# One VectorE instruction in place of two per expert tile: gate times up on GpSimd from a ScalarE copy, tanh written into the bank

## What is computed

```python
g = einsum('btd,edf->ebtf', x, gate_w)      # F = 192
u = einsum('btd,edf->ebtf', x, up_w)
h = silu(g) * u
expert_out = einsum('ebtf,efd->ebtd', h, down_w)
out = einsum('ebtd,bte->btd', expert_out, combine)
```

```python
state = state * exp(dt * A) + (dt * u) * B
y = einsum('bdn,bn->bd', state, C)
```

## Time and profile before

| | |
|---|---|
| median of 3 runs | 1610.0 us (1607.82 to 1610.88) |
| profiled execution, its own time | 1611.76 us |
| its span | 1610.0 us |
| mean granted TensorE clock | 0.925 of full speed |
| busy in the span | TensorE 87%, VectorE 59%, ScalarE 43%, GpSimd 47% |

### The profile page before, as it was taken

How to read it: one execution, slowest core, us unless ns; L and a number is a source line. 1 busy time by engine, 2 the same in 40 slices (tenths; PEclk the granted TensorE clock), 3 DMA queues, 4 the chain that set the end, 5 groups by cost and what they waited for, 6 DMA issues and landing times.

```text
span 1610.0 us, 18778 instructions
## 1 busy us (share of the span) xinstructions
PE 1396.8 (87%) x6080; PEld 1030.1 (64%) x6080; DVE 949.6 (59%) x1234; ACT 689.8 (43%) x1255; POOL 754.2 (47%) x559
## 2 busy tenths in 40 slices
PE   6988982599889889888175999999999999999998
PEld 3535531566556556555165787878788787878786
DVE  2767767999999999999584224241423224241413
ACT  4445433356666665665143333333333333333332
POOL 0000000877778778783631444444544445444542
PEclk9898895699999999999555999999999999999999
DMA  3202215477977887862664910020000100010000
GB/s 104 107 31 75 106 54 194 152 251 236 300 269 253 284 272 229 290 198 80 215 216 169 376 56 0 0 66 1 13 0 0 65 13 0 0 52 0 0 0 26
DMA packets 78200, 191.28 MB, mean 119 GB/s; under 512 B 10856, under 2 KB 15752, under 8 KB 77120
## 3 DMA queue, kind: packets, MB, share of 16 engines
q1 hardware_dynamic: 64832, 157.03, 28.5%
q0 software_dynamic: 6400, 20.98, 4.7%
q10 hardware_dynamic: 6912, 12.59, 2.1%
HBM read 152.55 MB, written 38.01 MB: 118 GB/s over the span
## 4 chain that ended last, share of the span: by engine, by line
PE 57%; DVE 25%; issue 9%; ACT 3%; DMA 3%; POOL 2%; ACTq 0%; SPq 0%; DVEq 0%; POOLq 0%
PE decay L1668 22%; PE bank L1657 21%; DVE decay L1235 14%; PE decay L1423 2%; PE bank L1467 2%; DVE XH L1102 2%; PE bank L1527 1%; PE bank L1487 1%; PE bank L1554 1%; PE bank L1430 1%; PE decay L1477 1%; DVE S L1244 1%; PE decay L1473 1%; PE bank L1437 1%; DVE HH L1255 1%
## 5 line engine op out<-in xcount | busy, mean ns | idle before, releaser
L723 POOL TENSOR_TENSOR S<-DTU,Bb 128x1024 f32<-128x1024 f32 x128 | 303.2, 2387 | 105.0 <-PE bank L1527 69.9
L1380 DVE CAST HFH<-HF 128x512 fp32r<-128x512 f32 x128 | 58.9, 460 | 497.2 <-ACT HF L1033 497.2
L805 POOL TENSOR_TENSOR W2L<-W2R,W2H 128x512 fp32r<-128x512 f32 x128 | 172.5, 1347 | 348.1 <-ACT W2H L1028 348.1
L1235 DVE TENSOR_TENSOR_SCAN decay<-decay,S 128x1024 f32<-128x1024 f32 x128 | 292.9, 2288 | 1.7 <-ACT decay L882 1.6
L1657 PE MATMUL bank<-XSH,W1H 128*128 128x512 f32 x512 | 203.4, 397 | 4.2 <-POOL W1L L801 4.2
L1668 PE MATMUL decay<-W2H,HFH 128*128 128x512 f32 x512 | 200.4, 391 | 5.0 <-DVE HFL L1382 5.0
L1657 PE MATMUL bank<-XSH,W1L 128*128 128x512 f32 x512 | 203.2, 397 | 0.0
L1657 PE MATMUL bank<-XSL,W1H 128*128 128x512 f32 x512 | 202.6, 396 | 0.0
L1668 PE MATMUL decay<-W2L,HFH 128*128 128x512 f32 x512 | 199.9, 390 | 0.0
L1668 PE MATMUL decay<-W2H,HFL 128*128 128x512 f32 x512 | 199.6, 390 | 0.0
L801 POOL TENSOR_TENSOR W1L<-W1R,W1H 128x512 fp32r<-128x512 f32 x128 | 171.0, 1336 | 47.7 <-ACT W1H L1019 47.7
(11 more groups left out here) (211 smaller groups left out, 2071.0 us busy)
## 6 DMA issues: line engine op xcount, KB each, us to landing
WGU<-in_L_ffn_gate_w SPq DMA_DIRECT2D x48, 384.0 KB
WGU<-in_L_ffn_up_w SPq DMA_DIRECT2D x48, 384.0 KB
WD<-in_L_ffn_down_w SPq DMA_DIRECT2D x48, 384.0 KB
Bb<-bc_rows SPq DMA_DIRECT2D x32, 512.0 KB, 6.5
Cb<-bc_rows SPq DMA_DIRECT2D x32, 512.0 KB, 8.6
expert_rows<-YT ACTq DMA_DIRECT2D x48, 256.0 KB
W1R<-in_L_ffn_w SPq DMA_DIRECT2D x6, 1024.0 KB, 13.7
W2R<-in_L_ffn_w SPq DMA_DIRECT2D x6, 1024.0 KB, 14.2
```

Of the source, the lines that this page charges most:

```text
L723: pool.tensor_tensor(S[u % NP][:], DTU[:, ds(b, 1), c, :].to_broadcast([P, PAIR, L]), Bb[j][:], ALU.mult).then_inc(dbu_ready, 1)
L805: pool.tensor_tensor(W2L[f % 2][:], W2R[:, ds(e, 1), f, :].rearrange("p e d -> p (e d)"), W2H[f % 2][:].bitcast(F32), ALU.subtract).then_i ...
L1235: dve.tensor_tensor_scan(flat, flat, S[u % NP][:].rearrange("p i l -> p (i l)"), 0.0, ALU.mult, ALU.add).then_inc(scan_done, 1)
```

## The change

- Buffers TG and HH (128x192 each, two of each) go; GU (128 x 2 x 192, two of it) comes: half 0 for the gate, half 1 for the up part.
- ScalarE, in `tanh_g`: it copies all 384 columns of UP to GU, waits for its own copy, and then writes tanh(g/2) over the gate columns of UP itself instead of into TG.
- GpSimd, new `gate_by_up(j)` behind the `dbu` of `units(j)` and ahead of the gather of tile j+2: it waits for that copy and multiplies g by u in GU (128x192, in place).
- VectorE: `gate_h` goes. `finish_h` waits for the tanh and for GpSimd's product, computes (UP + 1) * GU into GU, and stands between the scan and the read-out of the second unit, where `gate_h` stood; nothing of the experts stands behind that read-out.
- The factor 0.5 moves to the copy of DOWN into YT, which becomes an activation with scale 0.5.
- `turn_h` reads GU's half 0.

```diff
+            def gate_by_up(j):
+
+                pool.wait_ge(gu_copied, j + 1)
+                pool.tensor_tensor(GU[j % 2][:, 0], GU[j % 2][:, 0], GU[j % 2][:, 1], ALU.mult).then_inc(gg_ready, 1)
...
             for j in range(SLOT_TILES):
                 for u in units(j):
                     dbu(*bu(u))
+                gate_by_up(j)
                 if j + 2 < SLOT_TILES:
                     gather(0, j + 2)
...
             def tanh_g(j0, n):
                 act.wait_ge(up_ready, j0 + (n + 3))
-                act.activation(TG[n % 2][:], UP[:, 0:F], ACT.Tanh, scale=0.5).then_inc(tg_ready, 1)
+                act.copy(GU[n % 2][:].rearrange("p g f -> p (g f)"), UP[:, 0:2 * F]).then_inc(gu_copied, 1)
+                act.wait_ge(gu_copied, j0 + (n + 1))
+                act.activation(UP[:, 0:F], UP[:, 0:F], ACT.Tanh, scale=0.5).then_inc(tg_ready, 1)
...
-                act.copy(YT[:], DOWN[:]).then_inc(yt_ready, 1)
+                act.activation(YT[:], DOWN[:], ACT.Copy, scale=0.5).then_inc(yt_ready, 1)
...
-            def gate_h(j0, n):
+            def finish_h(j0, n):
 
                 dve.wait_ge(tg_ready, j0 + (n + 1))
-                dve.scalar_tensor_tensor(TG[n % 2][:], TG[n % 2][:], 1.0, UP[:, 0:F], ALU.add,
-                                         ALU.mult).then_inc(gg_ready, 1)
-
-            def finish_h(j0, n):
-
                 dve.wait_ge(gg_ready, j0 + (n + 1))
-                dve.scalar_tensor_tensor(HH[n % 2][:], TG[n % 2][:], 0.5, UP[:, F:2 * F], ALU.mult,
+                dve.scalar_tensor_tensor(GU[n % 2][:, 0], UP[:, 0:F], 1.0, GU[n % 2][:, 0], ALU.add,
                                          ALU.mult).then_inc(hh_ready, 1)
...
-            gate_h(0, 0)
             finish_h(0, 0)
             for j in range(SLOT_TILES):
                 for i, u in enumerate(units(j)):
                     scan(*bu(u))
                     if i == 1 and j + 1 < SLOT_TILES:
-                        gate_h(0, j + 1)
+                        finish_h(0, j + 1)
                     read_out(*bu(u))
-                    if i == 1 and j + 1 < SLOT_TILES:
-                        finish_h(0, j + 1)
```

More of the change, by code:

```diff
@@ L227, in build_program @@
         gcol = [sb(f, f"gcol{i}", [P, 1], I32) for i in range(2)]
-        TG = [sb(f, f"TG{i}", [P, F]) for i in range(2)]
-        HH = [sb(f, f"HH{i}", [P, F]) for i in range(2)]
+        GU = [sb(f, f"GU{i}", [P, 2, F]) for i in range(2)]
         HT = [sb(f, f"HT{i}", [FH, 2, P]) for i in range(2)]
@@ L375, in build_program @@
         gated = sem("gated")
+        gu_copied = sem("gu_copied")
         gt_ready = sem("gt_ready")
@@ L1558, in turn_h @@
             def turn_h(j0, n, last):
-                hh = HH[n % 2][:].rearrange("p (q k) -> p k q", k=2)
+                hh = GU[n % 2][:, 0].rearrange("p (q k) -> p k q", k=2)
                 pe.wait_ge(hh_ready, j0 + (n + 1))
```

## The result

The kernel with the change took **1597.2 us** (median of 6 runs, 1592.28 to 1601.36) against 1610.1 for the kernel before on the same chip (6 runs, 1607.82 to 1611.81). The ratio is 0.9922, 95% interval 0.9902 to 0.9942. The forecast was 1601.6, range 1596 to 1611. A second set of runs gave 0.9932 (0.9911 to 0.9952). A ratio here is not the quotient of the two medians: in the second set the medians, 1600.4 and 1609.1, differ by 8.7 us, which is 0.5%. So the kernel is faster by 0.5 to 0.8%, some 9 to 13 us where 8.4 were forecast.

A forecast was written before the change was run, and what follows sets the result against it. The prediction took VectorE, in the stage with scan and experts, to set the pace. Its terms, 12.0 - 2.3 - 1.35 = 8.35 us, took the median from 1610.0 to 1601.6 us, range 1596 to 1611.

The forecast's parts named there:

- The gain per tile: VectorE, units with a tile: freeing the place behind the read-out saves 0.25 us for each of 48 tiles, 12.0 us.
- the rival by busy time: VectorE: the instruction taken out brings its whole 0.34 us, 16.3 us before losses, giving 1597.3 us; chance 0.12.
- The prices of the new work: ScalarE's copy 0.47 us, GpSimd's product 0.68 (bounds 0.25 and 1.34), copy to finish 1.21 with handovers.
- Tile 1: Stage start: VectorE's finish stands 3.1 us for GpSimd's product, late behind a dbu; net loss 2.3 us.
- Tile 24: A store holds ScalarE, leaving 0.36 us between tanh and gate against 1.21 needed; 0.85 us lost.
- The few other tiles: Tiles with less than the usual 2.44 to 2.97 us of room before VectorE's finish; 0.5 us allowed together.
- The gather at nothing: GpSimd's gather, issued later behind the product, is late in the slowest cases only, by about 1 us; costed at nothing.
- ScalarE's copy at nothing: ScalarE gets some 24 us more work, covered by its 110.8 us of waiting for VectorE; otherwise a decay comes 0.5 later.
- Sum: Whole kernel: 12.0 gained, less 2.3 at the start and 1.35 at other tiles, gives 8.35 us.

The follow-up runs named there:

- experiments with more products: Changed kernel with one or two more 128x192 products per tile on GpSimd, results unused: 1598.3 us with one, 1614.8 us with two.
- The second copy: Changed kernel with ScalarE's copy of 384 columns from UP to GU made twice per tile: 1607.9 us, ratio 0.9988 to the kernel before.
- finish behind: Changed kernel with finish_h moved behind the read-out instead of between scan and read-out: 1604.2 us, ratio 0.9964 to the kernel before.
- early product: Changed kernel with GpSimd's product of tile 1 alone made ahead of that tile's last dbu: 1599.6 us, ratio 0.9933; repeated, 1597.2 us, 0.9927.
- gathers ahead: Changed kernel with the gather of tile j+2 ahead of the product of tile j in GpSimd's queue: 1603.4 us, ratio 0.9963.
- both moves: Changed kernel with tile 1's product ahead of that tile's last dbu and every gather ahead of the product on GpSimd: 1601.9 us, ratio 0.9950.

## Why the prediction was right, and where its steps missed

**The gain per tile: right.** 0.25 was forecast from start-to-start times, 0.26 came (3.84 to 3.58), and the rival by busy time, 0.34 and 16.3 us, is out: an instruction behind the read-out costs 0.27, one between scan and read-out 0.12, one in each 0.39. The prediction set against this the rule of the Trainium skill, "VectorE: DVE Perf Modes", section "The DRAIN you can't avoid", that the next instruction does not start until the pipe is empty, by which each instruction would be worth its whole duration. It left out that the same paragraph goes on: a next one that is not held starts earlier. The trace agrees with that second sentence: the finish, which has no wait for the scan, starts 2.19 us after a scan of 2.29.

**The prices of the new work: right.** Copy 0.48 (0.47 forecast), product 0.59 (0.68), from copy to finish at the five tiles where VectorE waited or nearly did 1.25 (1.21). GpSimd's round is 15.9 us and VectorE's 17.5, and the experiments with more products put the edge between a round of 17.2, which cost nothing in the median, and one of 18.4.

**Tile 1: right in place, the size set by the clock.** 3.1 us were forecast and 4.16 came. TensorE's up products took 5.31 us there against 4.44 in the profile that the forecast was read from, and the sums for which the last `dbu` waits come behind them. In the profiles with the product behind the tile's units and the finish in the gap the unit lost 1.5 to 4.7 us, 1.5 where the clock stayed up. The net loss at the start was forecast at 2.3; VectorE reaches unit 12 46.7 us after its first scan, before the change 44.6, so 2.1 late, and 2.6 with the half microsecond that two tiles should have brought. That this is near the forecast is luck in part, for the two profiles had different clocks there.

**Tile 24: right in place, and its size goes with the store.** A store held ScalarE ahead of this tile's copy in both profiles of the changed kernel, for 1.72 and 2.86 us, where it was 3.76 before:

```profile
528.32 0.60 ACT L912 ACTIVATE YT<-bank 128x512 f32<-128x512 f32 x1 [1.72 <-DMA expert_rows<-YT]
```

```profile
532.66 0.60 ACT L912 ACTIVATE YT<-bank 128x512 f32<-128x512 f32 x1 [2.86 <-DMA expert_rows<-YT]
```

The first used up all slack: the product ended 0.1 us ahead of the finish, and the unit took 3.65, so it lost 0.07. In the second profile the unit took 4.79 and lost 1.20, where it lost 1.06 in the kernel before. Twelve of the thirteen profiles with the change or a variant of it have a wait for the store there, of 0.2 to 2.9 us. It is a property of the kernel, and its length one of the run.

**The few other tiles: named too small.** 0.5 us were allowed. In the first profile tiles 6, 14, 22 and 38 lost 2.8 together, in the second tiles 6, 14, 18, 32 and 40 lost 5.1. The kernel before lost 2.8 at tiles 2, 8 and 32.

**The gather at nothing: right for the time, wrong for the wait.** It was late 15 times, not in the slowest cases only. Taking that away brought nothing.

**ScalarE's copy at nothing: the step that was least sound.** I named as cover the 110.8 us that ScalarE waits for VectorE, and as the one price a decay 0.5 later. The second copy shows another way: the take-out of the sums comes later, TensorE waits, and its next h and up come late. A second 0.5 us a tile costs 7 to 10.5 us of stage without any decay being late. The changed kernel's own wait at tile 22 (0.79) stands at the end of the same way; how much of its 7 and 11 us of waits in all (4 before) the first copy has by it was not separated.

**Sum.** In the stage 8.35 us were forecast, and 9.6 and 6.2 came in two profiles. The gain in the places was 47 x 0.26 = 12.2, where 12.0 were forecast, and the waits took back 7.3 - 3.9 = 3.4 and 10.6 - 3.9 = 6.7, where 3.65 were. That the 3.4 is so near is luck in part, since it came at other tiles than those that were priced. Another 0.7 came in both profiles at the units without a tile. The medians moved by 12.9 and 8.7. Some 3 us of the gain are therefore not accounted for by the stage. The part from the last scan to VectorE's first work in the feed-forward layer took 134.2 us before and 131.3 to 135.0 in the changed kernels, and the part ahead of the stage moves by up to 7 from run to run; with one profile of the kernel before, whether anything of this is the change's stays open.

## What to carry to other kernels

Price an instruction of a saturated in-order engine by start-to-start times with and without it, and by its place: here one that fills the gap in which its successor waits for its predecessor cost 0.12 of its 0.34 us, and one elsewhere 0.27. If two small instructions can become one, that is a reason to keep the one in the gap. An instruction that now waits for a chain over two other engines needs slack for the chain's bad cases, and the slack is lost by putting it early: here 1.3 us of it removed all waits but one, and cost in the stage as much as they did.

## What the runs showed of the hardware

Many of VectorE's waits stood behind a stretch in which TensorE's granted clock was lower. At tile 14 of the changed kernel TensorE waited 1.61 us for rows and 1.20 for a take-out, and its sums then took 3.47 us instead of 1.94:

```profile
430.25 0.75 PE L1547 MATMUL bank<-ident,XG 128*128 128x128 f32 x4 [1.61 <-DMA XG<-xn_rows,gcol]
...
432.19 3.47 PE L1527 MATMUL bank<-ident,S 128*128 128x128 f32 x16 [1.20 <-ACT U L929]
```

```profile
425.00:432.00 7.00, 4.38 (x24) 2.98 (x22) 6.93 (x5) 4.50 (x11) 5.42 (x5) 1.00 1.02 301
432.00:436.00 4.00, 3.81 (x17) 3.63 (x18) 4.00 (x4) 2.67 (x8) 3.72 (x3) 0.57 0.61 202
```

The clock fell to its lower level (1.2 of 2.4 GHz) for some 3.4 of these 4 us, after 7 in which TensorE was busy 4.4. In eight profiles of kernels without added work (before, changed twice, finish behind, early product twice, gathers ahead, both moves) I counted 38 units with a tile that lost over 0.3 us; in 30 of them the wait began in such a stretch or within 9 us behind one, while those spans of time make up 17 to 31% of the stage. That is a coincidence in time in 30 cases; the way from the one to the other was followed at tiles 14 and 22 and in the doubled copy only. At both tiles a wait of TensorE stood ahead of the lower clock, so the lower clock is not where the way begins.

The expectation for the repeated early product says that these stretches lie elsewhere in each run. That holds for some of them only. One began 139 to 145 us after the first scan in both profiles of the changed kernel, both with the early product, and the one with both moves, and in all five the unit with tile 14 lost 0.90 or 0.91 us. So that wait belongs to the place in the schedule. A learner who sees waits change from profile to profile should look for the ones that return.
